# Moving the second layer's preparation into the tail of the attention loop

## The reference, cut to what matters

```
h = relu(layernorm(x))
q, k, v = h @ Wq.T + bq, h @ Wk.T + bk, h @ Wv.T + bv
x = x + elu(softmax(where(adj > 0, q @ k.T / sqrt(128), NEG)) @ v)
h = relu(layernorm(x))                 # second layer starts here
hw = h @ W
s1, s2 = hw @ a[:128, 0], hw @ a[128:, 0]
att = softmax(where(adj > 0, leaky_relu(s1[:, None] + s2[None, :], 0.01), NEG))
out = x + hw + att @ h
```

## Time and profile before

| what | value |
|---|---|
| time, median of 3 runs | 781.47 us (781.42 to 786.33) |
| the profiled execution, its own time | 782.49 us |
| its span, first to last instruction | 780.7 us |
| mean granted TensorE clock | 0.977 |
| busy: TensorE, weight loads, VectorE, ScalarE, GpSimd | 728.9, 609.6, 563.2, 559.9, 417.6 us |
| second preparation's first and last instruction on VectorE | 495.47, 540.66 us |
| first and last matmul of the last block | 542.40, 774.2 us |

### The profile page before, as it was taken

The page is one execution under the profiler, slowest core; times in us unless marked ns, Lnnn a source line. Parts: engine busy times, 40 slices in busy tenths (PEclk is TensorE's granted clock), DMA queues, the critical chain, the costliest instruction groups (busy, mean ns, idle before and its releaser), DMA issues. The chain is left out here.

```text
span 780.7 us, 18250 instructions
## 1 busy us (share of the span) xinstructions
PE 728.9 (93%) x6229; PEld 609.6 (78%) x6229; DVE 563.2 (72%) x1199; ACT 559.9 (72%) x1095; POOL 417.6 (53%) x317
## 2 busy tenths in 40 slices
PE   4976999999999999999999998585999999999996
PEld 2555888888888888888888887463888888888885
DVE  4857687878787878878787876498585585586572
ACT  5936678687878777777868787584967977977910
POOL 1058599999999999999999973243000000000000
PEclk9988999999999999999999999797999999999999
DMA  6059989999888898989898954650234334423100
GB/s 229 1 162 280 283 212 248 274 232 280 233 280 238 271 253 254 262 247 256 255 259 245 274 112 73 123 103 1 54 69 93 81 73 91 91 64 87 37 10 13
DMA packets 189323, 130.86 MB, mean 168 GB/s; under 512 B 170336, under 2 KB 176992, under 8 KB 181088
## 3 DMA queue, kind: packets, MB, share of 16 engines
q1 hardware_dynamic: 188544, 130.05, 61.4%
q10 hardware_dynamic: 576, 0.26, 0.1%
q0 software_dynamic: 160, 0.00, 0.0%
HBM read 69.47 MB, written 18.87 MB: 113 GB/s over the span
## 5 line engine op out<-in xcount | busy, mean ns | idle before, releaser
L1337 PE MATMUL ps_x<-v,big 128*128 128x258 bf16 x2048 | 232.0, 275 | 2.3 <-issue 2.3
L1337 PEld LDWEIGHTS ps_x<-v,big 128*128 128x128 fp8e4 x2048 | 198.9, 98 | 32.5 <-issue 2.4
L682 DVE CUSTOM_DVE_ANT_0 scores<-ps_s,mask_neg 128x1024 f32<-128x1024 f32 x128 | 155.7, 1217 | 25.5 <-POOL mask_neg L553 17.0
L538 POOL TENSOR_SCALAR mask_bytes<-adj_sb 128x2048 uint8<-128x2048 int32 x64 | 147.5, 2321 | 44.8 <-POOLq L79 40.9
L601 ACT ACTIVATE scores<-scores,neg_max 128x1024 f32<-128x1024 f32 x128 | 146.1, 1143 | 23.3 <-DVE neg_max L688 23.3
L701 DVE TENSOR_TENSOR low<-scores 128x1024 bf16<-128x1024 f32 x96 | 136.0, 1417 | 29.2 <-ACT scores L601 27.0
L553 POOL TENSOR_SCALAR mask_neg<-mask_bytes 128x2048 bf16<-128x2048 uint8 x64 | 150.6, 2354 | 5.4 <-POOL mask_bytes L538 0.4
L812 PE MATMUL ps_acc<-v_parts,hiT 128*128 128x256 bf16 x768 | 141.6, 274 | 5.4 <-DMA lowT<-low 5.1
L615 ACT ACTIVATE hiT<-ps_t 128x512 bf16<-128x512 bf16 (+1 forms) x128 | 103.0, 805 | 56.6 <-PE ps_t L793 54.0
L878 ACT ACTIVATE big<-s_block,s_col 128x512 fp8e4<-128x512 f32 x224 | 139.3, 714 | 0.0
L813 PE MATMUL ps_acc<-v_parts,lowT 128*128 128x128 bf16 x768 | 134.7, 220 | 0.0
(11 more groups left out here) (139 smaller groups left out, 997.3 us busy)
## 6 DMA issues: line engine op xcount, KB each, us to landing
adj_sb<-in_adj SPq DMA_DIRECT2D x64, 1024.0 KB, 5.3
mask_bytes_dram<-mask_bytes SPq DMA_DIRECT2D x32, 512.0 KB, 2.8
x_sb<-in_x SPq DMA_DIRECT2D x8, 256.0 KB, 7.7
out<-res SPq DMA_DIRECT2D x32, 64.0 KB, 1.5
lowT<-low SPq DMA_TRANSPOSE x96, 4.7
big<-mask_bytes_dram SPq DMA_TRANSPOSE x32, 4.5
raw_w<-in_L_gnn_Wq ACTq DMA_DIRECT2D x1, 64.0 KB, 3.1
raw_w<-in_L_gnn_Wk ACTq DMA_DIRECT2D x1, 64.0 KB, 3.6
```

What stands on the lines that cost most here:

```text
L538: nc.gpsimd.tensor_scalar(mask_bytes[b % 2][:, half(h)], adj_sb[h][:], 1.0, 0.0, ALU.min, ALU.max).then_inc(bytes_ready, 1)
L682: nc.vector.tensor_tensor_reduce(out=scores[bn % 2][:, part(k)], in0=ps_s[k % 2][:], in1=mask[bn % 2][:, part(k)], scale=1.0, scalar=LOWES ...
L1337: last = nc.tensor.matmul(ps_x[b % 2][k][:], by_key_tile(m, t)[:, b], v1[k][:, t, :].bitcast(BF16), start=(t == 0), stop=(t == T - 1))
```

## The change

The second preparation has no block of its own any more. Its instructions stand in the attention block, in each engine's own order:

- The buffers that the second layer needs are laid over those of the loop: the normalised h over the two halves of the adjacency rows, its transpose `hT2` over `scores[0]`, the weighed words `v1` over q, the row of s1 over the masks, and the four mask buffers over k, `scores[1]` and v. PSUM is shared in the same way.
- The roots and the reciprocal go: VectorE makes the inverse root from an integer seed and three Newton steps, all tiny instructions, 24 tiles in periods 28 and 29 (`variance`, `inverse_root`), 4 tiles in period 30, the last 4 after the loop. The two table loads go with the roots.
- The normalisation of chunks 0 to 6 goes from VectorE to GpSimd (24 tiles in period 30, 4 in period 31); the last chunk stays on VectorE.
- `turn_h`, `s_products` and `hw_product` on TensorE, `hT_out` and `s_out_of` on ScalarE, `weigh` and `add_hw` on VectorE and `split_words` on GpSimd are the old steps. Chunks 0 to 2 stand partly between the steps of strip 31, the rest after them. The negated s2 comes out of the product with a third column of `wa`.
- Sign bytes are first made for strips 0 and 1 alone: of each chunk's four tiles ScalarE writes two, VectorE one and GpSimd one, 256 columns each. The other half, strips 2 and 3, is written in the last block: 10 tiles by VectorE, 22 by GpSimd. `cut(0, 0, 2)` waits for both (`late_signs`).
- The product h @ W of chunks 4 to 7 is made after the maxima; its additions to x stand at the start of the last block on VectorE, behind its 10 tiles of bytes. The last of them (c = 7) waits for `add_hw(3)`, VectorE's last instruction in the block.
- SyncE starts the eight mask loads behind the last `turn_low`, four of them after the last scores and four after the last turns.

```diff
...
+        v1 = [q_parts[:, T * (D + 1) * i:T * (D + 1) * (i + 1)].rearrange("p (t f) -> p t f", f=D + 1) for i in range(2)]
+        h_sb = adj_both[:].bitcast(F32).rearrange("p (t f) -> p t f", f=D)
+        hT2 = scores[0]
+        s1_row = mask_both[:].bitcast(F32)
+        big = [over_k[0][:], scores[1][:].bitcast(U32), over_k[1][:],
+               v_parts[:].rearrange("p t k f -> p (t k f)").bitcast(U32)]
+        upper, lower = big[0:2], big[2:4]
...
+        def compare_bytes(engine, par, src, t, strips):
+            return engine.tensor_scalar(by_key_tile(lower[par], t, U8)[:, strips], strips_of(src, strips),
+                                        s_col[:, t, 2:3], 128.0, ALU.is_lt, ALU.mult)
...
+                    sp.wait_ge(s_ready, 4 * T)
+                    for b in range(4):
+                        load_mask(sp, 0, b, 0)
+                    sp.wait_ge(t_done, TURNS * T)
+                    sp.wait_ge(low_done, 3 * T)
+                    for b in range(4):
+                        load_mask(sp, 1, b, 1)
...
+                    def normalise(c):
+                        for t in range(4 * c, 4 * c + 4):
+                            last = nc.gpsimd.tensor_scalar(h_sb[:, t, :], x_sb[:, t, :], stats["moments"][:, t, 0:1],
+                                                           stats["rstd"][:, t:t + 1], ALU.subtract, ALU.mult)
+                        last.then_inc(h_ready, 1)
...
+                    def early_sign(c):
+                        pool.wait_ge(s1_out, 1)
+                        pool.wait_ge(s_out, c + 1)
+                        compare_bytes(nc.gpsimd, 0, s1_row, 4 * c + 3, EARLY).then_inc(pool_signs, 1)
...
+                        if last_ones and s == T - 1:
+                            pool.wait_ge(rstd_ready, 2)
+                            normalise(6)
...
+                        if last_ones and s == T - 2:
+                            pool.wait_ge(bytes_ready, 2 * T)
+                            pool.wait_ge(rstd_ready, 1)
+                            for n in range(6):
+                                normalise(n)
...
+                    split_words(0)
                     add_elu(T - 2)
+                    split_words(1)
                     add_halves(T - 1)
+                    split_words(2)
                     add_elu(T - 1)
+                    for c in range(3):
+                        early_sign(c)
+                    for c in range(3, NC):
+                        early_sign(c)
+                        split_words(c)
...
+                        if not ahead:
+                            act.wait_ge(low_done, 3 * T - 3)
+                            hT_out(0)
...
                     all_periods(act, period)
+                    hT_out(2)
+                    s_out_of(1)
+                    hT_out(3)
                     acc_copy(T - 1, 3)
+                    s_out_of(2)
                     elu_exp(T - 1)
-                    use_table(1, ACT.Sqrt)
...
+                    early_signs(0)
+                    for c in range(3, NC):
+                        hT_out(c + 1) if c + 1 < NC else None
+                        s_out_of(c)
+                        early_signs(c - 2)
+                    for c in range(NC - 2, NC):
+                        early_signs(c)
...
+                    def variance(cs):
+                        bn, moments, spread = stats["bn"][:, cs], stats["moments"][:, cs], newton[:, 0, cs]
+                        mean_e, mean_o, m2_e, m2_o = (bn[:, :, i] for i in (1, 4, 2, 5))
+                        mean, var = moments[:, :, 0], moments[:, :, 1]
+                        dve.wait_ge(bn_done, cs.stop)
+                        tail.mark(nc.vector.tensor_tensor(stats["root"][:, cs], mean_e, mean_o, ALU.subtract))
+                        tail.mark(nc.vector.tensor_tensor(mean, mean_e, mean_o, ALU.add))
+                        tail.do(nc.vector.tensor_tensor(var, m2_e, m2_o, ALU.add))
+                        tail.mark(nc.vector.scalar_tensor_tensor(out=spread, in0=stats["root"][:, cs], scalar=0.25,
+                                                                 in1=stats["root"][:, cs], op0=ALU.mult, op1=ALU.mult))
+                        tail.mark(nc.vector.tensor_scalar(mean, mean, 0.5, None, ALU.mult))
+                        tail.do(nc.vector.tensor_scalar(var, var, 1.0 / D, EPS, ALU.mult, ALU.add))
+                        tail.do(nc.vector.tensor_tensor(var, var, spread, ALU.add))
+                    def inverse_root(cs):
+                        var, rstd, square = stats["moments"][:, cs, 1], stats["rstd"][:, cs], newton[:, 1, cs]
+                        tail.do(nc.vector.tensor_scalar(seed[:, cs], var.bitcast(I32), 1, None, ALU.logical_shift_right))
+                        tail.do(nc.vector.tensor_scalar(rstd.bitcast(I32), seed[:, cs], -1.0, MAGIC, ALU.mult, ALU.add))
+                        for _ in range(3):
+                            tail.do(nc.vector.tensor_tensor(square, rstd, rstd, ALU.mult))
+                            tail.do(nc.vector.scalar_tensor_tensor(out=square, in0=square, scalar=-0.5, in1=var,
+                                                                   op0=ALU.mult, op1=ALU.mult))
+                            ins = nc.vector.scalar_tensor_tensor(out=rstd, in0=square, scalar=1.5, in1=rstd,
+                                                                 op0=ALU.add, op1=ALU.mult)
+                            tail.do(ins)
...
+                        if isinstance(c, int) and s == T - 4:
+                            variance(slice(0, 24))
+                        if isinstance(c, int) and s == T - 3:
+                            inverse_root(slice(0, 24))
+                            nc.vector.sem_inc(rstd_ready, 1)
+                        if isinstance(c, int) and s == T - 2:
+                            variance(slice(24, 28))
+                            inverse_root(slice(24, 28))
+                            nc.vector.sem_inc(rstd_ready, 1)
...
+                    dve.wait_ge(epi_done, T - 2)
+                    moments_of(T - 3)
+                    weigh(0)
+                    early_sign(0)
+                    weigh(1)
+                    early_sign(1)
+                    dve.wait_ge(epi_done, T - 1)
+                    moments_of(T - 2)
+                    weigh(2)
+                    early_sign(2)
+                    weigh(3)
+                    dve.wait_ge(epi_done, T)
+                    moments_of(T - 1)
+                    variance(slice(28, 32))
+                    inverse_root(slice(28, 32))
+                    for t in range(28, 32):
+                        last = nc.vector.tensor_scalar(h_sb[:, t, :], x_sb[:, t, :], stats["moments"][:, t, 0:1],
+                                                       stats["rstd"][:, t:t + 1], ALU.subtract, ALU.mult)
+                    last.then_inc(h_last, 1)
+                    early_sign(3)
+                    for c in range(4, NC - 1):
+                        weigh(c)
+                        early_sign(c)
+                        add_hw(c - 4)
+                    dve.wait_ge(s_out, NC)
+                    tail.mark(nc.vector.tensor_reduce(out=hT_total[:], in_=hT_sum[:], axis=AX.X, op=ALU.add))
+                    nc.vector.tensor_reduce(out=top[:, 0:1], in_=s_col[:, :, 1], axis=AX.X, op=ALU.max)
+                    tail.do(nc.vector.tensor_reduce(out=top[:, 1:2], in_=s_col[:, :, 0:2], axis=AX.XY, op=ALU.max,
+                                                    apply_absolute_value=True))
+                    nc.vector.tensor_scalar(hT_diag[:], ident[:], hT_total[:], None, ALU.mult).then_inc(top_ready, 1)
+                    weigh(NC - 1)
+                    early_sign(NC - 1)
+                    dve.wait_ge(words_in[0], 64)
+                    scale_mask(0, 0).then_inc(scaled_ready, 1)
+                    dve.wait_ge(top_t, 1)
+                    nc.vector.tensor_copy(h_sum[:], ps_s2[:, D:2 * D])
+                    tail.do(nc.vector.tensor_reduce(out=top_turned[:], in_=ps_s2[0:2, 0:D], axis=AX.X, op=ALU.max))
+                    nc.vector.tensor_scalar(top_diag[:], ident[0:2, 0:2], top_turned[:], None, ALU.mult).then_inc(top_d, 1)
+                    dve.wait_ge(scaled_ready, 1)
+                    dve.wait_ge(signs_ready, 1)
+                    dve.wait_ge(vector_signs, NC)
+                    dve.wait_ge(pool_signs, NC)
+                    cut_lower(0, 0).then_inc(lower_ready, 1)
+                    dve.wait_ge(top_b, 1)
+                    tail.do(nc.vector.tensor_copy(top[:], ps_s2[:, 0:2]))
+                    tail.do(nc.vector.tensor_scalar(flag[:], top[:, 1:2], SAFE, None, ALU.is_le))
+                    dve.wait_ge(lower_ready, 1)
+                    cut_upper(0, 0).then_inc(parts_ready, 1)
+                    add_hw(3)
...
+                        if not ahead:
+                            pe.wait_ge(masked, 4 * T)
+                            turn_h(0)
```

(41 more changed lines are left out.)

400 lines of the change are left out of this document (182 added, 218 removed).

## The result

The changed kernel takes 801.25 us in the median (800.88 to 802.26, 4 runs), the kernel before 783.9 (781.42 to 786.67): a ratio of 1.0222, 95% interval 1.0175 to 1.027, so it is slower. The prediction was 771.1, faster. The profiled execution has a span of 800.5 and its own time is 802.26, against 780.7 and 782.49.

A forecast was written before the change was run, and what follows sets the result against it. TensorE alone bounds the last block, so its start counts: x 504.3 + VectorE 18.3 + port 5.5 + 1.1 + 2.5 + 1.6 = 533.3. With 229.8 + 1.0 + 6.2 the span is 770.3, median 771.1, range 762 to 785.

The forecast's parts named there:

- The step that failed: GpSimd's prices: 0.35 for a normalisation (bounds 0.29 and 0.46), 0.48 for a 256-column tile of bytes.
- Late bytes: Last block, strip 2: GpSimd's 22 tiles take 10.6, the mask is ready at 15.6, stall 1.0 (bounds 0 and 5.5).
- The last rows of x: Strip 31 and the queues behind it: x complete at 504.3, against 494.83 before.
- Newton parts at nothing: Periods 28 to 30: tiny steps and normalisations lie beside waits, costed at nothing beyond 0.8; at most 3.5 for period 30.
- VectorE behind x: VectorE's chain from x complete to add_hw(3): work without a gap, sum 18.3.
- the port: Behind x, VectorE waits for GpSimd's instruction in flight, less 0.12: 5.5 in all, bounds 0 and 9.2.
- Rival 1: VectorE and GpSimd sharing the port costs next to nothing and GpSimd is quick (0.29): 762.8; chance 0.15.
- rival 2: Port held for the whole recorded instruction, some 60 waits 0.12 longer: 778.5; chance 0.18, including GpSimd at its dearer price.
- To the first strip: From VectorE's end to the last block's first strip: TensorE 1.1 behind, lowered clock 2.5, change of blocks 1.6.
- Rival 3: GpSimd pays for column operands, 1.0 per normalisation and 1.2 per byte tile: 807; decides from 0.52 and 0.70; chance 0.13.

The follow-up runs named there:

- fast_pairs: Changed kernel with GpSimd's normalisation as add, mult on a negated mean and its comparison as add, mult into bytes, nothing moved: 778.18 us, ratio 0.9907.
- quiet_pool: Changed kernel with GpSimd's eight early comparisons on ScalarE and the low words of chunks 3 to 7 set to zero: 793.75 us, ratio 1.0096.
- var_later: Changed kernel with the variances of tiles 0 to 23 moved from strip 28's period to strip 29's: 800.55 us, ratio 1.0185.
- fast_x_first: Changed kernel with the cheap pairs of operations and the last rows of x put ahead in three engines' queues: 778.98 us, ratio 0.9917.
- price: Changed kernel plus 120 TENSOR_SCALAR instructions on GpSimd beside the last block, varying columns and column operands; run once, 802.19 us, not used.
- price2: A second price list on GpSimd beside the last block: thirteen more groups of six, varying operation pair, input type and length; run once, 804.69 us, not used.

## Why the prediction was wrong

**The step that failed is one price.** "A plain one takes 1.89 for 2048 columns ... at one column in 0.83 ns": I took the price of min, max and of mult, add for subtract, mult and is_lt, mult, and called the two rows that I had its bounds. They bound nothing for another pair of operations: the two forms took 0.787 and 1.14. With the cheap pairs in place the measured prices are 0.444 and 0.508 against my 0.35 and 0.48. Changing the pairs alone took away 23.1 of the 30.1 between forecast and result. The rest of the way, fast_pairs' span of 776.6 against 770.3, is 3.1 of mark, 3.0 of x, 1.0 of VectorE, 0.9 less to the first strip and 0.1 behind it.

**Late bytes.** Ready at 15.6 with a stall of 1.0 was the forecast. GpSimd's 22 tiles took 27.0 in place of 10.6, and the stall was 14.0, with 1.5 more while the clock came back (384 matmuls in 44.59, where six strips are 43.1). In fast_pairs the 22 tiles took 12.7 and the stall was 1.1. This is 14.5 of the miss.

**The last rows of x.** From the mark 113.2 in place of 101.9. fast_pairs has 104.9, so 8.3 are GpSimd's price, 2.5 the longer period, and 0.5 is left for the rest of the sum (my 0.35 against 0.444, the three `turn_h`, the queues on ScalarE and GpSimd). How these divide was not measured.

**Newton parts at nothing.** Wrong by 2.5. I had named their length as the cost without cover (3.5 for one part) but not the part in strip 28, where small VectorE instructions of 0.2 waited up to 1.7 for GpSimd's mask bytes. This is the wait that I had read in the earlier trace rows; for VectorE I had counted it only behind x.

**VectorE behind x, and the port.** 25.7 against 18.3 + 5.5. Without GpSimd it is 18.6, of which 0.5 wait for ScalarE, so the plain sum was right to 0.3 and the port was 7.1 to 7.6, not 5.5. Rival 1 (the port costs next to nothing) is refuted by that; rival 2's longer waits were not measured apart. The 0.41 that I gave to the 512-column comparison stands in no row; nothing hangs on it, for in quiet_pool a 256-column comparison took 0.26 from its start to the next one's, where I took 0.28.

**To the first strip.** TensorE behind VectorE 3.1 (forecast 3.6) and the block change 1.36 (1.6); the clock fell as I had written.

**The sum.** 770.3 + 2.7 (mark) + 11.3 (x) + 1.9 (VectorE) - 0.7 (to the first strip) + 13.0 (stall) + 1.5 (clock) = 800.0; the span was 800.5. Of the 2.7, 0.5 lie in the loop's steady part (402.43 - 96.07 = 306.4 in before, 405.16 - 98.27 = 306.9 in after, 23 periods each). The rest lies ahead of it, and is smaller than the 6.6 between the marks of kernels whose loops are the same up to there, so no run ties it to the change.

**Rival 3** gave 807 at prices of 1.0 and 1.2, and a deciding point of 0.52 and 0.70; the prices were 0.79 and 1.14, and the kernel was slower. Its direction was right and its prices were too high by 0.2 and 0.06; its reason was wrong: column operands are 0.075 each, near the 0.085 that the estimate from the Trainium skill's GPSIMD Engine Reference (Performance pitfalls for Q7 kernels) gave for one. With 0.13 I gave it too little, for the trace had no row of either form on GpSimd, which I had said myself. A slip that changes nothing: three quarters of 0.54 and 0.15 are 0.555, not 0.57.

**Not settled.** Why a subtract costs four times an add on GpSimd. How the 1.6 that remains in var_later divides between the dependent steps and what they push. What an is_lt in the second place costs, and whether other operations are dear.

## What to carry to other kernels

A duration may be carried from one instruction to another only at the same engine and the same pair of operations; here the pair alone was a factor of four for each column. Type (f32 or bytes) made no difference, and size counted only through the number of columns. That one price took the kernel from 2.2% slower than before to 0.9% faster (801.25 and 778.18 us). Where a change puts a form on an engine that the trace has never seen there, give the case "several times dearer" a real chance, and first look for an equivalent form that the trace has (x + (-mean) for x - mean). Moving work ahead of a shared resource's other user can take back what it wins: in fast_x_first x came 5.7 earlier, and VectorE's waits behind it grew by 5.0.

## What the hardware showed that I had not expected

- GpSimd's TENSOR_SCALAR: 0.21 us plus 3.33 ns a column with subtract, mult; mult, subtract; or is_lt, mult (0.637 at 128, 1.917 at 512 columns). It is 0.19 plus 0.83 ns with mult, add or min, max (0.292 and 0.616); subtract, mult has the same 1.917 on f32 and on bytes (price, price2). Add, mult has 0.44 at 128 with two column operands (fast_pairs).
- A column operand adds 0.075, once for an instruction, at 128 columns and at 512 (price).
- VectorE's smallest instructions grow most by the port: one of 0.16 took 1.04 beside split_words (fast_x_first), and one of 0.20 took 1.94 beside a 1.9-us mask instruction (after).
